# First linear of a graph kernel: the bias added by VectorE on the way out of PSUM, instead of by bias products on TensorE and copies on ScalarE

## The chip, the core and the metric

The kernel runs on 1 core of one Trainium2 chip. The metric is the device time of one execution in microseconds (us). Before the change three runs took 533.06, 533.36 and 534.27 us; their median is 533.36 us.

## The reference, cut to what matters

Four sublayers follow one another on 1250 nodes of 512 features with 40,000 edges: a graph attention with 8 heads, a gated linear with an expert picked for the whole batch, a graph convolution, and a mixture of 8 experts. The change is in the first linear of the first sublayer:

```python
def _L0_gnn_ref(x, edge_index, Ws, Wb, a_w, a_b):
    for h in range(8):
        Wx = x @ Ws[h] + Wb[h]                  # 1250 x 512 times 512 x 64, plus a bias
        s = Wx[v_tgt] @ a_w[h, :d] + Wx[v_src] @ a_w[h, d:] + a_b[h]
        s = leaky_relu(s, 0.2)
        alpha = segment_softmax(s, v_tgt, n)
        outs.append(segment_sum(alpha[:, None] * Wx[v_src], v_tgt))
...
x = x + _L0_gnn_ref(_layernorm(x), edge_index, ...)
```

## The kernel before, in words

The nodes lie in T = 10 tiles of 128. The attention needs a dense 1280 x 1280 matrix of edge counts, `C` and `C2`, and the kernel builds it first, in a loop over 160 pairs of edge chunks (20 batches `b` of LB = 8 pairs). For each pair i:

- VectorE writes one-hot matrices, for half a batch (4 pairs) at a time: `half_left` (L1033) and `half_right` (L1039), both recorded at L1019. Half u = 2b + half makes the pairs 4u to 4u+3. It may be at most 16 pairs ahead: `half_left(u)` waits until pair 4u-12 is counted.
- TensorE multiplies them in `count` (two matmuls, L1598), and `merge` (L1605) adds the old counts through the identity.
- ScalarE copies the 180 counts of a window back into `C` or `C2` (`write_batch`, L605). `merge(i)` waits for the writes of the pairs up to i-2.

The first linear is worked into this loop, one tile for every STEP = 12 pairs. Tile t begins at pair LIN_AT[t] = 16 + 12t. Before that, ScalarE normalises its rows (L574), TensorE transposes them (L1509), ScalarE copies the transposed tile as f16 at pair LIN_AT[t]-8 (L566), and VectorE makes the low part of the f16 split (`xT_low`, L938) in half LIN_AT[t]/4. In that same half VectorE calls `ln_scale` (L932, L933) for tile t+1, which waits for a square root that ScalarE takes at pair LIN_AT[t+1]-20, that is LIN_AT[t]-8 (L561). In the half after it comes `ln_stats` for tile t+2 (L915 to L917), as long as there is such a tile.

At each of the 12 pairs from LIN_AT[t] on, TensorE's `lin_a(t, j)` adds one product to two sums: 128 x 512 outputs in bank 2 + t % 2 (L1557, the values `Wx`) and 128 x 16 in bank 4 + t % 2 (L1558, the scores `sc`). Weights are scaled by WS = 256 and split into a high and a low f16 part. At j = 0 it first opens both sums with a bias product: 64 rows holding 1/32, times `Wb16` (L1553) or `cb16` (L1554), whose rows 0 to 63 hold high parts of the bias, with rows 32 to 63 turned into low parts. Before them it waits for `xT_ready` and, as the banks alternate, for `evacA` of tile t-2:

```python
                    pe.wait_ge(sem("xT_ready"), t + 1)
                    if t >= 2:
                        pe.wait_ge(sem("evacA"), t - 1)
```

At pair LIN_AT[t]+12 ScalarE takes both sums out of PSUM, in `evac_a` (L597 and L598).

The bias halves are made once. After batch 0 ScalarE writes the high parts (L677, L679, after a wait for all small loads, `ld_w1`), and after batch 1 VectorE subtracts them from the bias (L1109, L1110).

At the last batch VectorE computes `scores` (L963 to L966). TensorE transposes the thresholds at pair 146 (L1573), VectorE copies them out (L1076) behind its last one-hots, SP writes them to DRAM (L381) and reads them back broadcast (L386). When all counts are written (`hist_done`, L690) VectorE joins `C` and `C2` (L1147), and the aggregation of the heads begins; ScalarE's masks (L697) are the first to read the thresholds.

Of the kernel before, what the change touches and what calls it, by code (L numbers as in the profile page):

```python
# [8 lines left out]
F16 = mybir.dt.float16  # L9
# [59 lines left out]
ROWS_P = {LIN_AT[t] - 9: t for t in range(T)}  # L69
COPY_P = {LIN_AT[t] - 8: t for t in range(T)}  # L70
LIN_P = {LIN_AT[t] + j: (t, j) for t in range(T) for j in range(STEP)}
EVAC_P = {LIN_AT[t] + STEP: t for t in range(T)}
XT0 = 4
AHEAD = 3
EPS = 1e-5
# [3 lines left out]
def gnn_ffn_kernel(nc, x_d, src_d, dst_d, Ws_d, Wb_d, aw_d, ab_d, Wg_d, bg_d, We_d, be_d, gW_d, gb_d,  # L79
                   Wr_d, br_d, W1_d, b1_d, W2_d, b2_d, out_d):  # L80
    ctx = ExitStack()
    with ctx:
# [92 lines left out]
        ones16, o = carve(mid, o, [P], F16)  # L175
        minusT16, o = carve(mid, o, [P], F16)
        span_i, o = carve(mid, o, [2, HG], I32)
        part32, o = carve(mid, o, [2], F16)
        num_words = num[:, :, :].rearrange("p h f -> p (h f)")
        lo16, o = carve(num_words, 0, [RE], F16)  # L180
        hi16, o = carve(num_words, o, [RE], F16)
        src_i = be_bc[:, 0:RE].bitcast(I32)
        Wb16, o = carve(be_bc, 0, [D], F16)
        cb16, o = carve(be_bc, o, [2 * H], F16)
        VP, o = carve(big, 0, [T, 2, H, 2, FE], F16)
        nacc, o = carve(big, o, [T, H, FE])

# [263 lines left out]
        def _(g):  # L451
# [15 lines left out]
            nc.gpsimd.iota(iota_lo, [[1, P]], base=0, **kw)  # L467
            nc.gpsimd.memset(ones16, 1.0)
            nc.gpsimd.memset(minusT16, -float(T))
            nc.gpsimd.memset(part32, 1.0 / 32)  # L470
            nc.gpsimd.iota(iota_q, [[1, RW]], base=1, **kw).then_inc(sem("consts"), 1)
            nc.gpsimd.memset(zero[:, 0, :], 0.0).then_inc(sem("consts"), 1)
            nc.gpsimd.iota(iota8[:, :], [[1, E1]], base=-99, **kw)
# [82 lines left out]
        def _(a):  # L556
# [34 lines left out]
                if i == 3:  # L591
                    act(A2, e2t, ACT.Exp).then_inc(sem("exps"), 1)

            def evac_a(t):

                a.wait_ge(sem("linA"), t + 1)
                act(Wx[:, t, :, 0:F], bank[2 + t % 2][:, :].rearrange("p (h f) -> p h f", h=H), ACT.Copy, scale=1.0 / WS)  # L597
                act(sc[:, t, :], bank[4 + t % 2][:, 0:2 * H], ACT.Copy, scale=1.0 / WS).then_inc(sem("evacA"), 1)  # L598

            def write_batch(base, at, middle):  # L600

                for k in range(LB):
# [48 lines left out]
            for b in range(NB):  # L651
                def middle(k):
                    i = b * LB + k
                    if i in SQRT_P:
                        ln_sqrt(SQRT_P[i])
                    if i in EVAC_P:
                        evac_a(EVAC_P[i])
                    if i in NORM_P:
                        t = NORM_P[i]
                        ln_norm(t, x[:, t, :], xh_ring[:, t % 2, :])  # L660
                    if k == LB - 3 and b + 1 < NB:
                        at.append(targets(mybir.EngineType.Activation, (b + 1) * LB))
                    if b == NB - 1 and k <= 3:
                        exponential(k)
                    if b == NB - 1 and k == 4:
                        act(sd[0:1, 0:1], zero16[0:1, 0:1], ACT.Sigmoid)
                    if i in COPY_P:
                        t = COPY_P[i]
                        if t >= 2:
                            a.wait_ge(sem("linA"), t - 1)  # L670
                        ln_copy(t, bank[6], xTs[:, t % 2, 0, :, :])

                write_batch(b * LB, at[b], middle)
                if b == 0:
                    a.wait_ge(sem("wa_psum"), 1)
                    act(Wa[:, 0, :, :].rearrange("p k c -> p (k c)"), bank[5][:, 0:K * 2 * H], ACT.Copy, scale=WS)
                    act(cb16[0:64, :], bank[5][0:64, K * 2 * H:(K + 1) * 2 * H], ACT.Copy, scale=WS)  # L677
                    a.wait_ge(sem("ld_w1"), 128)
                    act(Wb16[0:64, :], Wb_bc[0:64, :, :].rearrange("p h f -> p (h f)"), ACT.Copy, scale=WS).then_inc(sem("weight_hi"), 1)  # L679
            n = a.value_load(npass[0:1, 0:1], min_val=1, max_val=MAXPASS)  # L680
            with a.If(n > 1):
                with a.Fori(1, n) as p:
# [219 lines left out]
        def _(v):  # L902
# [156 lines left out]
            def value(h):  # L1059

                if h:
                    v.wait_ge(sem("v_lo"), h)
                V.tensor_tensor(vtmp, Wx[:, :, h, :].unsqueeze(1).to_broadcast([P, 2, T, FE]),
                                bc(B12[:, :, :, h], [P, 2, T, FE]), ALU.mult).then_inc(sem("v_made"), 1)

            def tile_step(u):
                if u in SCALE_H:
                    ln_scale(SCALE_H[u])
                if u in LOW_H:
                    t = LOW_H[u]  # L1070
                    xT_low(t, bank[6], xTs[:, t % 2, :, :, :])
# [10 lines left out]
            pair_tables(0, first_stats)  # L1082
            for b in range(NB):
                if b == NB - 1:
                    scores()
                    last_onehots(b)
                    threshold_rows()
                elif b:
                    for half in range(2):
                        u = 2 * b + half  # L1090
                        if u in STATS_H:
                            if STATS_H[u] == XT0:
                                v.wait_ge(sem("ld_x"), 32)
                            ln_stats(STATS_H[u], x[:, STATS_H[u], :])
                        half_left(b, half)
                        tile_step(u)
                        half_right(b, half)
                else:
                    first_onehots()
                    ln_scale(0)  # L1100
                    v.wait_ge(sem("weight_hi"), 1)
                    V.scalar_tensor_tensor(W016[:, 1, :, :], W0.rearrange("p k h f -> p k (h f)"), WS, W016[:, 0, :, :],
                                           ALU.mult, ALU.subtract).then_inc(sem("weight_lo"), 1)
                if b == 1:
                    passes()
                    v.wait_ge(sem("weight_hi"), 2)
                    V.scalar_tensor_tensor(Wa[:, 1, :, :].rearrange("p k c -> p (k c)"), bank[5][:, 0:K * 2 * H], WS,
                                           Wa[:, 0, :, :].rearrange("p k c -> p (k c)"), ALU.mult, ALU.subtract)
                    V.scalar_tensor_tensor(cb16[32:64, :], bank[5][32:64, K * 2 * H:(K + 1) * 2 * H], WS, cb16[32:64, :], ALU.mult, ALU.subtract)  # L1109
                    V.scalar_tensor_tensor(Wb16[32:64, :], Wb_bc[32:64, :, :].rearrange("p h f -> p (h f)"), WS, Wb16[32:64, :],  # L1110
                                           ALU.mult, ALU.subtract).then_inc(sem("weight_lo"), 1)
            v.wait_ge(sem("exps"), 4)
            v.wait_ge(sem("xp_zeroed"), 16)
            V.memset(cz[:, :, NODES:NP], 0.0)
# [389 lines left out]
        def _(pe):  # L1504
# [39 lines left out]
            def lin_a(t, j):  # L1544
                k, i = divmod(j, len(PASSES))
                xp, wp = PASSES[i]
                if j == 0:
                    if t == 0:
                        pe.wait_ge(sem("weight_lo"), 2)
                    pe.wait_ge(sem("xT_ready"), t + 1)  # L1550
                    if t >= 2:
                        pe.wait_ge(sem("evacA"), t - 1)
                    mm(bank[2 + t % 2][:, :], part32[0:64, 0:1].to_broadcast([64, P]), Wb16[0:64, :], start=True, stop=False)  # L1553
                    mm(bank[4 + t % 2][:, 0:2 * H], part32[0:64, 0:1].to_broadcast([64, P]), cb16[0:64, :], start=True, stop=False)  # L1554
                xt = xTs[:, t % 2, xp, k, :]
                last = j == K * len(PASSES) - 1
                mm(bank[2 + t % 2][:, :], xt, W016[:, wp, k, :], start=False, stop=last)  # L1557
                ins = mm(bank[4 + t % 2][:, 0:2 * H], xt, Wa[:, wp, k, :], start=False, stop=last)  # L1558
                if last:
                    ins.then_inc(sem("linA"), 1)  # L1560

# [418 lines left out]
```

## Time and profile before

| | |
|---|---|
| median of 3 runs | 533.36 us (533.06 to 534.27) |
| the profiled execution | 534.08 us, of which 532.3 us are its span (first to last instruction) |
| mean granted TensorE clock | 0.979 |
| TensorE matmul busy | 486.5 us, 91% of the span |
| VectorE busy | 423.5 us, 80% |
| ScalarE busy | 341.2 us, 64% |
| GpSimd busy | 82.9 us, 16% |

The shares are means over stages with different limits. The change lies in the counting loop, between about 27 and 128 us, so that stretch has to be read by itself. PE is TensorE, PEld its weight loads, DVE VectorE, ACT ScalarE, POOL GpSimd, SP the queue that starts most transfers. A row of the timeline gives the start, the length, the engine and the line, and in brackets the idle time before it with the instruction that ended it. Successive rows of one engine may overlap by up to a tenth of a us, as the end of one instruction lies over the beginning of the next.

### The profile page before, as it was taken

Reading aid. Unit: us, or ns where it says so; the run is one execution under the profiler, and the core shown is the slowest. Engines: PE = TensorE matmul, PEld = TensorE weight load, DVE = VectorE, ACT = ScalarE, POOL = GpSimd, SP = SyncE. Lnnn points to the kernel's source line nnn. Section 1 sums busy time; section 2 is a strip of 40 time slices with the busy share of each in tenths; the row PEclk is TensorE's granted clock in tenths of the full one; section 3 lists DMA queues with packets and bytes.
Section 4 is the critical chain, followed back from the end, with each engine's and each line's share of the span. In section 5 each row is a group of like instructions: output and inputs, shape, how many; then the busy total and the mean of one; then the engine's idle time right before and its main releaser. Section 6 shows DMA issues by size and latency. Waiting matters only on the chain.

```text
span 532.3 us, 11466 instructions
## 1 busy us (share of the span) xinstructions
PE 486.5 (91%) x4389; PEld 359.9 (68%) x4390; DVE 423.5 (80%) x856; ACT 341.2 (64%) x657; POOL 82.9 (16%) x95
## 2 busy tenths in 40 slices
PE   3989999993899999999999899889899999999995
PEld 3866666762898999998787544444466697776662
DVE  7878778685999999966888778985877787886781
ACT  7467677668799999972766723435345558867630
POOL 5000000000000000001121201223244511222322
PEclk9889999999799999999999999999999999999999
DMA  8970000003011111002000294000011119965201
GB/s 201 323 262 1 1 2 1 2 2 102 2 50 52 52 54 64 37 1 80 1 2 1 89 324 161 1 0 4 0 42 42 61 60 347 379 224 184 91 28 55
DMA packets 25267, 45.10 MB, mean 85 GB/s; under 512 B 6977, under 2 KB 7013, under 8 KB 25212
## 3 DMA queue, kind: packets, MB, share of 16 engines
q1 hardware_dynamic: 23228, 39.16, 21.5%
q0 software_dynamic: 1952, 5.18, 2.7%
q8 instruction: 37, 0.61, 0.5%
q14 instruction: 18, 0.15, 0.1%
q10 hardware_dynamic: 32, 0.01, 0.0%
HBM read 33.23 MB, written 11.95 MB: 85 GB/s over the span
## 4 chain that ended last, share of the span: by engine, by line
PE 33%; DVE 21%; issue 6%; DMA 5%; ACT 4%; POOL 4%; POOLq 0%; DVEq 0%
PE sums L1697 13%; PE sums L1531 7%; PE sums L1710 5%; PE sums L1922 3%; DMA aux<-xperm_scratch 2%; POOL row L532 2%; DVE st L915 2%; DVE big L1324 2%; DMA out<-aux 2%; DVE work L1161 2%; PE sums L1509 1%; POOL out L516 1%; ACT rings L574 1%; DVE aux L1446 1%; PE sums L1687 1%
## 5 line engine op out<-in xcount | busy, mean ns | idle before, releaser
L1697 PE MATMUL sums<-big,work 128*128 128x130 f16 x1080 | 67.2, 225 | 8.0 <-DVE work L1161 7.9
L1697 PEld LDWEIGHTS sums<-big,work 128*128 128x128 f16 x1080 | 64.5, 100 | 9.6 <-issue 6.2
L1019 DVE TENSOR_TENSOR big<-mid 128x1024 f16<-128x1024 f16 (+1 forms) x88 | 59.4, 735 | 1.5 <-PE sums L1605 1.4
L1598 PE MATMUL sums<-big 128*128 128x180 f16 x320 | 59.4, 270 | 0.3 <-DVE big L1019 0.3
L1798 PE MATMUL sums<-mid 128*128 128x512 f16 x200 | 47.2, 378 | 0.0
L1710 PE MATMUL sums<-big,mid 128*128 128x260 f16 x400 | 47.0, 275 | 0.1
L1557 PE MATMUL sums<-big,rings 128*128 128x512 f16 x120 | 45.4, 378 | 0.0
L1710 PEld LDWEIGHTS sums<-big,mid 128*128 128x128 f16 x400 | 38.2, 96 | 7.5 <-issue 0.3
L605 ACT ACTIVATE mid<-sums 128x180 f32 x80 | 26.5, 332 | 25.5 <-PE sums L1605 24.8
L697 ACT ACTIVATE aux<-aux,small 128x1250 f16<-128x1250 f32 x32 | 40.9, 1326 | 2.5 <-DVE work L1161 1.7
L697 ACT ACTIVATE mid<-aux,small 128x1250 f16<-128x1250 f32 x32 | 40.8, 1324 | 2.4 <-DVE work L1161 2.4
L561 ACT ACTIVATE sd<-ve 128x1 f32<-128x1 f32 x40 | 8.0, 200 | 50.9 <-DVE ve L917 50.9
L1598 PEld LDWEIGHTS sums<-big 128*128 128x128 f16 x320 | 37.5, 120 | 3.9 <-issue 0.7
L493 POOL TENSOR_TENSOR row<-row,mid 128x512 f32<-128x512 f32 x9 | 10.6, 1177 | 162.5 <-DVE mid L1228 162.5
L915 DVE BATCH_NORM_STATS2 st<-row 128x6 f32<-128x512 f32 x40 | 27.6, 691 | 9.4 <-POOL row L532 7.8
L605 ACT ACTIVATE big<-sums 128x180 f32 x80 | 26.2, 327 | 12.9 <-PE sums L1605 11.0
L516 POOL DMA_INDIRECT out<-aux x16 | 23.1, 1446 | 70.6 <-DVE aux L1446 68.2
L1697 PE MATMUL sums<-big,rings 128*128 128x130 f16 x520 | 31.6, 220 | 0.7 <-DVE rings L1161 0.7
L574 ACT ACTIVATE rings<-row,nm,rs 128x512 f32<-128x512 f32 x30 | 24.3, 809 | 12.3 <-DVE nm L933 12.3
L1798 PEld LDWEIGHTS sums<-mid 128*128 128x128 f16 x200 | 19.7, 104 | 18.0
L1697 PEld LDWEIGHTS sums<-big,rings 128*128 128x128 f16 x520 | 29.9, 98 | 1.3 <-DVE rings L1161 1.1
L1605 PE MATMUL sums<-big,ident 128*128 x80 | 26.2, 328 | 2.9 <-ACT big L605 2.9
(330 smaller groups left out, 1099.6 us busy)
## 6 DMA issues: line engine op xcount, KB each, us to landing
big<-in_L_ffn_W SPq DMA_DIRECT2D x10, 1024.0 KB, 14.2
mid<-in_L_ffn_W SPq DMA_DIRECT2D x6, 1024.0 KB, 13.8
xperm_scratch<-work SPq DMA_DIRECT2D x1, 5753.0 KB, 18.7
aux<-thr_scratch SPq DMA_DIRECT2D x8, 640.0 KB, 3.9
aux<-xperm_scratch SPq DMA_DIRECT2D x8, 523.0 KB, 4.5
row<-in_x SPq DMA_DIRECT2D x1, 1280.0 KB
aux<-in_L_gnn_Ws SPq DMA_DIRECT2D x4, 256.0 KB, 4.6
row<-in_x SPq DMA_DIRECT2D x1, 1024.0 KB, 6.5
```

Source lines behind the costliest of these rows:

```text
L516: nc.gpsimd.indirect_dma_start(out_d, bass.IndirectOffsetOnAxis(ap=ids[0:m, r, j:j + 1], axis=0), xs[0:m, r, j, 0:D], None, bounds_check=N ...
L574: act(dst, xt, ACT.Identity, bias=nm[:, n % 2:n % 2 + 1], scale=rs[:, n % 2:n % 2 + 1]).then_inc(sem("xh_made"), 1)
L605: ins = act(counts_at(at[k], k), count_bank(base, k)[:, 0:RW].rearrange("p (d s) -> p s d", s=T), ACT.Copy)
L697: act(dst, thr_bc[:, h % 2, 0:NODES], ACT.Sigmoid, bias=steep[:, s, h:h + 1], scale=-STEEP).then_inc(sem("z_made"), 1)
L915: link(V.bn_stats(st[:, i, :], xt))
L1019: return V.tensor_tensor(out.rearrange("p c (v two) -> p c v two", two=2), values.rearrange("p (v two) -> p v two", two=2).unsqueeze(1).to ...
L1531: ins = mm(out, xt16[:, xp, k, :], w16[:, wp, k, :], start=i == 0 and k == 0, stop=i == 2 and k == K - 1)
L1557: mm(bank[2 + t % 2][:, :], xt, W016[:, wp, k, :], start=False, stop=last)
L1598: mm(count_bank(base, k)[:, 0:RW], L_ring[:, slot, k * CH + j, :], R_ring[:, slot, k * CH + j, :], start=j == 0, stop=False)
L1697: ins = mm(acc_region(h, t), weighted[i // 2 % NC][:, s % 2, t * P:(t + 1) * P], VP[:, s, part, h, :, :].rearrange("p b f -> p (b f)"), st ...
L1710: ins = mm(edge_bank(t, g2)[:, 0:4 * FE].rearrange("p (h f) -> p h f", f=FE), C[:, s, t * P:(t + 1) * P], VP[:, s, part, 4 * g2:4 * g2 + 4 ...
L1798: ins = mm(bank[6 + t % 2][:, :], C[:, s, t * P:(t + 1) * P], hp[:, s, part, :], start=s == 0 and part == 0, stop=s == T - 1 and part == 1)
```

## The change

The two bias products, `part32`, `Wb16` and `cb16` go away, and so does `evac_a` on ScalarE. ScalarE copies the score bias `cb` out of bank 5 as f32. The first product of each tile opens the sums. VectorE takes the tiles out in a new function, `linear_out`: one scalar_tensor_tensor of 128 x 512 and one of 128 x 16, each (sum x 1/WS) + bias, from PSUM to SBUF in f32.

```diff
-EVAC_P = {LIN_AT[t] + STEP: t for t in range(T)}
+EVAC_H = {(LIN_AT[t] + STEP + 16) // HALF: t for t in range(T - 1)}
...
-            def evac_a(t):
-                a.wait_ge(sem("linA"), t + 1)
-                act(Wx[:, t, :, 0:F], bank[2 + t % 2]..., ACT.Copy, scale=1.0 / WS)
-                act(sc[:, t, :], bank[4 + t % 2][:, 0:2 * H], ACT.Copy, scale=1.0 / WS).then_inc(sem("evacA"), 1)
...
                     act(Wa[:, 0, :, :]..., bank[5][:, 0:K * 2 * H], ACT.Copy, scale=WS)
-                    act(cb16[0:64, :], bank[5][0:64, K * 2 * H:(K + 1) * 2 * H], ACT.Copy, scale=WS)
-                    a.wait_ge(sem("ld_w1"), 128)
-                    act(Wb16[0:64, :], Wb_bc[0:64, :, :]..., ACT.Copy, scale=WS).then_inc(sem("weight_hi"), 1)
+                    act(cb, bank[5][:, K * 2 * H:(K + 1) * 2 * H], ACT.Copy).then_inc(sem("weight_hi"), 1)
...
+            def linear_out(t):
+                v.wait_ge(sem("linA"), t + 1)
+                V.scalar_tensor_tensor(Wx[:, t, :, 0:F], bank[2 + t % 2]..., 1.0 / WS, Wb_bc, ALU.mult, ALU.add)
+                V.scalar_tensor_tensor(sc[:, t, :], bank[4 + t % 2][:, 0:2 * H], 1.0 / WS, cb, ALU.mult, ALU.add).then_inc(sem("evacA"), 1)
...
                 if b == NB - 1:
+                    linear_out(T - 1)
                     scores()
...
                             ln_stats(STATS_H[u], x[:, STATS_H[u], :])
+                        if u in EVAC_H:
+                            if EVAC_H[u] == 0:
+                                v.wait_ge(sem("ld_w1"), 128)
+                            linear_out(EVAC_H[u])
                         half_left(b, half)
...
-                    V.scalar_tensor_tensor(cb16[32:64, :], ...)
-                    V.scalar_tensor_tensor(Wb16[32:64, :], ...).then_inc(sem("weight_lo"), 1)
...
-                    mm(bank[2 + t % 2][:, :], part32[0:64, 0:1].to_broadcast([64, P]), Wb16[0:64, :], start=True, stop=False)
-                    mm(bank[4 + t % 2][:, 0:2 * H], part32[0:64, 0:1].to_broadcast([64, P]), cb16[0:64, :], start=True, stop=False)
-                mm(bank[2 + t % 2][:, :], xt, W016[:, wp, k, :], start=False, stop=last)
-                ins = mm(bank[4 + t % 2][:, 0:2 * H], xt, Wa[:, wp, k, :], start=False, stop=last)
+                mm(bank[2 + t % 2][:, :], xt, W016[:, wp, k, :], start=j == 0, stop=last)
+                ins = mm(bank[4 + t % 2][:, 0:2 * H], xt, Wa[:, wp, k, :], start=j == 0, stop=last)
```

`EVAC_H` puts the tiles 0 to 8 at the halves 11, 14, ..., 35. Tile t's sums are thus taken out in the half that makes the pairs LIN_AT[t]+28 to LIN_AT[t]+31; in the halves 11 to 26 this stands right behind an `ln_stats`, and in all of them before the one-hots. Tile 9 is taken out just before `scores`.

## Rows read from the trace of the kernel before

**Rows 1.** Windows (us, busy us of PE, PEld, DVE, ACT, POOL, granted clock, DMA share, GB/s).
```profile
42.20:50.29 8.09, 7.74 (x68) 5.49 (x67) 6.30 (x13) 5.58 (x18) 0.00 (x0) 1.00 0.00 0
...
113.11:128.20 15.09, 10.17 (x80) 6.94 (x79) 8.79 (x25) 11.02 (x33) 0.45 (x1) 1.00 0.29 91
128.20:240.00 111.80, 101.86 (x1642) 97.30 (x1643) 106.94 (x96) 103.62 (x87) 0.00 (x0) 0.95 0.10 38
```

**Rows 2.** Timeline of PE around the bias products of tile 1.
```profile
41.56 0.38 PE L1557 MATMUL sums<-big,rings 128*128 128x512 f16 x1
...
42.20 0.39 PE L1553 MATMUL sums<-be_bc,mid 64*128 64x512 f16 x1
...
42.53 0.39 PE L1557 MATMUL sums<-big,rings 128*128 128x512 f16 x1
...
43.09 0.38 PE L1557 MATMUL sums<-big,rings 128*128 128x512 f16 x1
```

**Rows 3.** Timeline of VectorE, one tile's round and the beginning of the next.
```profile
46.19 0.16 DVE L932 RECIPROCAL rs<-sd 128x1 f32<-128x1 f32 x1 [1.56 <-ACT sd L561]
...
46.68 0.69 DVE L938 TENSOR_TENSOR rings<-sums,rings 128x512 f16<-128x512 f32 x1
47.29 0.90 DVE L1019 TENSOR_TENSOR big<-mid 128x1440 f16<-128x1440 f16 x1
48.10 0.69 DVE L915 BATCH_NORM_STATS2 st<-row 128x6 f32<-128x512 f32 x1
...
49.11 3.52 DVE L1019 TENSOR_TENSOR big<-mid 128x1024 f16<-128x1024 f16 x5
54.16 0.16 DVE L932 RECIPROCAL rs<-sd 128x1 f32<-128x1 f32 x1 [1.53 <-ACT sd L561]
...
57.08 3.52 DVE L1019 TENSOR_TENSOR big<-mid 128x1024 f16<-128x1024 f16 x5
```

**Rows 4.** Timeline of PE: the bias products of the tiles 2 and 3 begin.
```profile
50.29 0.39 PE L1553 MATMUL sums<-be_bc,mid 64*128 64x512 f16 x1
...
58.17 0.39 PE L1553 MATMUL sums<-be_bc,mid 64*128 64x512 f16 x1
```

**Rows 5.** By source line: durations (ns min/median/max) of like instructions on VectorE.
```profile
L1446 DVE SCALAR_TENSOR_TENSOR aux<-sums,small,aux x16: 735/750/753, 448.9 to 525.8; 128x512 f32<-128x512 f32 x8, 80x512 f32<-80x512 f32 x8
...
L1107 DVE SCALAR_TENSOR_TENSOR small<-sums,small x1: 225/225/225, 27.9 to 27.9; 128x64 f16<-128x64 f32 x1
```

**Rows 6.** Timeline of ScalarE and PE where tile 9's sums are taken out.
```profile
113.36 0.59 ACT L597 ACTIVATE mid<-sums 128x512 f32<-128x512 f32 x1
...
113.53 0.33 PE L1605 MATMUL sums<-mid,ident 128*128 x1
...
114.35 0.33 PE L1605 MATMUL sums<-big,ident 128*128 x1 [0.34 <-ACT big L605]
```

**Rows 7.** Timeline from the last halves to the join: VectorE, PE, SP, ScalarE; and the landing times of L386.
```profile
110.31 1.51 DVE L1019 TENSOR_TENSOR big<-mid 128x1024 f16<-128x1024 f16 x2 [0.66 <-PE sums L1605]
112.60 1.51 DVE L1019 TENSOR_TENSOR big<-mid 128x1024 f16<-128x1024 f16 x2 [0.77 <-PE sums L1605]
114.06 0.24 DVE L963 TENSOR_TENSOR small<-small 128x80 f32<-128x80 f32 x1
...
118.89 1.60 DVE L1076 COPY rings<-sums 8x512 f32<-8x512 f32 x3
...
128.16 2.30 DVE L1147 TENSOR_TENSOR mid<-mid,big 128x1280 f16<-128x1280 f16 x3 [2.04 <-ACTq L690]
...
117.77 1.25 PE L1573 MATMUL sums<-ident,small 128*8 128x128 f32 x10
...
122.46 0.81 SPq L386 DMA_DIRECT2D aux<-thr_scratch  x2
...
129.48 2.55 ACT L697 ACTIVATE mid<-aux,small 128x1250 f16<-128x1250 f32 x2
...
DMA to landing us min/median/max: 3.5/3.9/5.5
```

More of the change, by code:

```diff
@@ L177, in gnn_ffn_kernel @@
         span_i, o = carve(mid, o, [2, HG], I32)
-        part32, o = carve(mid, o, [2], F16)
         num_words = num[:, :, :].rearrange("p h f -> p (h f)")
@@ L182, in gnn_ffn_kernel @@
         src_i = be_bc[:, 0:RE].bitcast(I32)
-        Wb16, o = carve(be_bc, 0, [D], F16)
-        cb16, o = carve(be_bc, o, [2 * H], F16)
         VP, o = carve(big, 0, [T, 2, H, 2, FE], F16)
@@ L469, in _ @@
             nc.gpsimd.memset(minusT16, -float(T))
-            nc.gpsimd.memset(part32, 1.0 / 32)
             nc.gpsimd.iota(iota_q, [[1, RW]], base=1, **kw).then_inc(sem("consts"), 1)
@@ L592, in exponential @@
                     act(A2, e2t, ACT.Exp).then_inc(sem("exps"), 1)
-            def evac_a(t):
-                a.wait_ge(sem("linA"), t + 1)
-                act(Wx[:, t, :, 0:F], bank[2 + t % 2][:, :].rearrange("p (h f) -> p h f", h=H), ACT.Copy, scale=1.0 / WS)
-                act(sc[:, t, :], bank[4 + t % 2][:, 0:2 * H], ACT.Copy, scale=1.0 / WS).then_inc(sem("evacA"), 1)
             def write_batch(base, at, middle):
@@ L655, in middle @@
                         ln_sqrt(SQRT_P[i])
-                    if i in EVAC_P:
-                        evac_a(EVAC_P[i])
                     if i in NORM_P:
@@ L676, in _ @@
                     act(Wa[:, 0, :, :].rearrange("p k c -> p (k c)"), bank[5][:, 0:K * 2 * H], ACT.Copy, scale=WS)
-                    act(cb16[0:64, :], bank[5][0:64, K * 2 * H:(K + 1) * 2 * H], ACT.Copy, scale=WS)
-                    a.wait_ge(sem("ld_w1"), 128)
-                    act(Wb16[0:64, :], Wb_bc[0:64, :, :].rearrange("p h f -> p (h f)"), ACT.Copy, scale=WS).then_inc(sem("weight_hi"), 1)
+                    act(cb, bank[5][:, K * 2 * H:(K + 1) * 2 * H], ACT.Copy).then_inc(sem("weight_hi"), 1)
             n = a.value_load(npass[0:1, 0:1], min_val=1, max_val=MAXPASS)
@@ L1064, in value @@
                                 bc(B12[:, :, :, h], [P, 2, T, FE]), ALU.mult).then_inc(sem("v_made"), 1)
+            def linear_out(t):
+                v.wait_ge(sem("linA"), t + 1)
+                V.scalar_tensor_tensor(Wx[:, t, :, 0:F], bank[2 + t % 2][:, :].rearrange("p (h f) -> p h f", h=H), 1.0 / WS,
+                                       Wb_bc, ALU.mult, ALU.add)
+                V.scalar_tensor_tensor(sc[:, t, :], bank[4 + t % 2][:, 0:2 * H], 1.0 / WS, cb, ALU.mult, ALU.add).then_inc(sem("evacA"), 1)
             def tile_step(u):
@@ L1107, in _ @@
                     V.scalar_tensor_tensor(Wa[:, 1, :, :].rearrange("p k c -> p (k c)"), bank[5][:, 0:K * 2 * H], WS,
[L1108 to L1111, printed above, removed]
+                                           Wa[:, 0, :, :].rearrange("p k c -> p (k c)"), ALU.mult, ALU.subtract).then_inc(sem("weight_lo"), 1)
             v.wait_ge(sem("exps"), 4)
```

## The prediction

> **What bounds the kernel now.** I read the page's table of busy time first and only to see that no single engine is the answer: the shares mix stages. Then I cut the span into windows. The change lies between 27 and 128 us, and one tile's stretch of it, from one bias product to the next, has TensorE busy 7.74 of 8.09 us, VectorE 6.30 and ScalarE 5.58, at the full granted clock (1.00, the 2.4 GHz level) [rows 1]. So TensorE sets the pace there. The timeline of PE says how: one pair's work (one product each of L1557 and L1558, a merge, two counts) repeats every 0.56 us (42.53 to 43.09) with no gap of its own, and the one irregular step is the first of each tile, where 0.97 us pass from 41.56 to 42.53 [rows 2]. VectorE's timeline shows the opposite: once per tile it stands idle for about 1.5 us until ScalarE's square root at L561 [rows 3], and ScalarE does that in its order behind a write that waits for TensorE. VectorE is thus ahead, tied to TensorE's pace once per round, with a margin. The view of waits shows no wait of TensorE for VectorE in this stretch, and waits for ScalarE only behind pair 136. The chain that ended last is of no use here: it can be followed back only to 143 us.
>
> **The bias products.** Per tile the products of L1553 and L1554 go. From the first one's start to the first real product, 42.20 to 42.53, it is 0.33 us [rows 2]. The step as a whole is 0.97 - 0.56 = 0.41 us too long; the other 0.08 us lie before the bias product, where TensorE's queue passes the waits for `xT_ready` and `evacA`, and those stay. I take 0.33. The lower bound: a regular step moves 3 x 180 + 512 + 16 = 1068 columns in 0.56 us, so the 528 columns of the bias cost 0.28 us if only the columns count. The upper bound is 0.41. With 10 tiles: 3.3 us, between 2.8 and 4.1. Nothing covers this, because TensorE has no idle time here that it could fall into.
>
> **VectorE's new work.** Before, VectorE's round lasts 54.16 - 46.19 = 7.97 us, of which 1.53 are idle: 6.44 us of work [rows 3]. TensorE's rounds at the same place are 58.17 - 50.29 = 7.88 us and, in the window above, 8.09 us; the two kinds alternate [rows 4]. The change puts into each round one scalar_tensor_tensor of 128 x 512 from PSUM with an f32 operand in SBUF, and one of 128 x 16. The nearest rows: 0.75 us for the same operation and shape at L1446, and 0.225 us for 128 x 64 at L1107, an upper bound for 16 columns [rows 5]; L938, which also reads 512 columns of PSUM and a second tensor, has 0.69 [rows 3]. Successive instructions on VectorE overlap by about 0.08 us (0.69 from 46.68, but the next starts at 47.29). So the pair takes 0.75 - 0.08 + 0.225 - 0.08 = 0.81 us of the round, between 0.7 (by L938) and 0.98 (no overlap). The round's work becomes 7.25 us against a round of TensorE of 7.97 - 0.33 = 7.64. VectorE still arrives early, by 0.39 us, and the work is hidden by that idle time. If that cover were gone, each us over it would be added to the round.
>
> **The new wait on TensorE.** This is the place where the change can bite. `lin_a` of tile t+2 waits for `evacA` of tile t, which ScalarE gave one whole round earlier and VectorE now gives late. For the tiles 0 to 5 VectorE reaches `linear_out` behind `ln_stats`. In the old timeline that is 49.11 us, where the one-hots now start, and TensorE wants the bank at 50.29; in the next round it is 57.08 and 58.17 [rows 3, 4]. Both are counted from the same ScalarE step, with no bias product between, so the distances (1.18 and 1.09 us) stay. The pair is done 0.75 - 0.08 + 0.225 = 0.90 us after it starts. That leaves 0.28 and 0.19 us, less some hundredths for the semaphore and 0.08 because TensorE's queue handles its waits just before. I count no wait, and at most 0.1 us for each of 6 tiles. Queued behind such a wait are the next merges and counts, so all of the loop would be late with it. The tiles 6 to 8 have no `ln_stats` before them and are 1.0 us better off. The wait of `linear_out` itself, on `linA`, is on a sum that was finished a round before (tile 0 at 42.2 us, read at 49.1), so it stops nobody; at tile 9 the sum is finished at 113 us and VectorE comes after 114.
>
> **ScalarE.** It loses 10 times 0.59 us and a small copy. In the rounds it had idle time, so that gives nothing, except at tile 9: there the write of a window waits behind L597 from 113.36 on, and the merge at 114.35 stands idle for 0.34 us [rows 6]. That goes: -0.34. The copies of the bias halves go also (ScalarE once 0.63 and 0.17 us after batch 0, VectorE about 0.8 us after batch 1), at a point where VectorE waits over 2 us for the round behind it: nothing.
>
> **The end of the loop.** VectorE takes tile 8 and tile 9 out just where its idle times are 0.66 and 0.77 us. The tiles 7 and 8 cost 1.62 us and use these up, and tile 9 another 0.81: scores start about 1.0 us late, 1.3 counted from the pair on TensorE that is 0.33 us earlier, and 1.7 if the 0.34 at tile 9 comes too. Scores began at 114.06, the first thresholds are ready half a us later, and TensorE asks for them only at 117.77, so 3.2 us of cover are enough. VectorE copies the thresholds out after its last one-hots, now up to 1.7 us late; the load issued at 122.46 lands 3.5 to 5.5 us later, as a rule 3.9, so with the delay at 128.1, and the first mask that reads it starts at 129.48 (129.1 after the gain at tile 9). Hidden, by 1.0 us. What follows, the join at 128.16, waits for the last write of ScalarE alone, and VectorE is then busy 106.94 of 111.80 us [rows 7, 1]: each us won before the join is won at the end.
>
> **The sum.** -3.3 - 0.34 = -3.64 us. On the profiled execution that is 534.08 - 3.64 = 530.44 us (span 528.7); it lay 0.72 us above the median, so for the median 533.36 - 3.64 = 529.7 us.
>
> **A rule that speaks against it.** The Trainium skill, in Perfetto Trace Analysis, section Optimizing Scalar/DVE Operations, gives VectorE a larger fixed cost on PSUM (about 125 ns) than ScalarE (about 51 ns) and advises to shift work to ScalarE where VectorE is saturated. The trace agrees on the first point (0.69 to 0.75 us against 0.59), and by the rule the change goes the wrong way: VectorE is the busier of the two. Were VectorE saturated, the gain would shrink as in the first rival below.
>
> **The rivals.**
> - *VectorE becomes the bound of the round.* It needs a pair of 1.20 us (7.64 - 6.44), against 0.98 at the worst from rows. For it speaks only that the margin shrinks from 1.5 to 0.4 us. Then the rounds with statistics keep about their old length and only tiles 0, 1, 8 and 9 and the 0.34 give anything: 4 x 0.33 + 0.34 = 1.7 us, 531.7. Chance 0.07.
> - *TensorE waits for the bank in six tiles.* The margin is 0.1 to 0.2 us by my reckoning. If the pair takes 0.2 us longer, or the semaphore does, TensorE loses about 0.1 to 0.25 us six times, 0.6 to 1.5 us: 530.3 to 531.2. Chance 0.15.
> - *The thresholds come late.* The first load of L386 is the one that lands after 5.5 us: then it is there at 129.7, 0.6 us after the mask wants it: 530.3. With a further us of delay 531.3. Chance 0.05.
> - *The products were covered after all:* the step's length is that of the waits, and TensorE only stands there instead. For it: the queue's 0.08 us. Against it: 0.33 us between two product starts. Only 0.34 us are left, 533.0, no measurable change. Chance 0.05.
> - *Slower: the wait for the bank, large.* Same place as the second, but the pair of 0.9 us slips by a whole one-hot product or more (0.90 us, L1019), or VectorE is slowed in PSUM while TensorE writes other banks. From 0.79 us a tile on, six times, it eats the 3.64 us and 1.07 more; at 0.9 us of wait the time is 533.36 - 3.64 + 5.4 = 535.1. Against it: L938 reads PSUM in the midst of TensorE's writes in 0.69 us, the same every time. Chance 0.06.
>
> **How the numbers follow.** The forecast itself has 0.62, with its own range from 528.4 (4.1 for the bias, 0.34, and half a us from ScalarE's free time elsewhere) to 530.6 (2.8). To hold 8 in 10 the range takes in the second and third rival and the first: 528.2 to 531.9 us. A measurement of this kernel tells about 0.2% from no change, 1.07 us. Faster by more than that, below 532.3 us, are the forecast and the first three: 0.89, of which I take 0.04 away for what I have not thought of: 0.85. Within it 0.08, slower 0.07.
>
> **What would show it.** In the profile after: the round of TensorE 7.55 and 7.76 us instead of 7.88 and 8.09; L1557 of each tile starting where L1553 did, with no idle time before it that ends on VectorE; the new operations on VectorE at about 0.75 and 0.2 us; VectorE's idle time before L932 at 0.3 to 0.5 us instead of 1.53; no idle time of 0.34 us near tile 9; the join at about 124.5 instead of 128.16 us, and everything after it the same length. Wrong it would be if TensorE shows a wait on the new line's semaphore in the tiles 2 to 7, if VectorE has no idle time left before L932, if ScalarE's first mask waits for a load, or if the stretch behind the join has grown.

## The result, and the profile after

The changed kernel takes 532.0 us (median of 20 runs, 527.97 to 535.06). In the same measurement the kernel before, of which three runs had given 533.36, came to 536.95 us over 20 runs (533.06 to 539.18). The ratio is 0.9922, with a 95% interval from 0.9899 to 0.9945: 4.2 us less, between 3.0 and 5.4. (The means over all runs, 531.99 and 536.16 us, give this ratio; the two medians lie 4.95 us apart.) The forecast difference was 3.64 us. The forecast time of 529.7 us was 2.3 us too low, and 532.0 lies 0.1 us above the upper end of the range.

The profiled execution of the changed kernel took 533.77 us with a span of 532.0 us, only 0.3 us less than before. Each trace is one execution: that of the kernel before (534.08 us) was among its faster ones, that of the changed kernel among its slower ones. One has to look where those 532.0 us lie. First the windows of the changed kernel, from its merge 16 (the pair at which tile 0 begins) to the join and from the join to the end; columns as in [rows 1].

```profile
36.71:126.90 90.19, 83.11 (x717) 60.77 (x716) 75.67 (x153) 59.79 (x178) 0.45 (x1) 1.00 0.05 16
126.90:532.00 405.10, 377.21 (x3518) 278.45 (x3518) 326.83 (x655) 256.89 (x421) 73.63 (x66) 0.98 0.23 82
```

The same two stretches of the kernel before:

```profile
33.86:128.16 94.30, 86.83 (x736) 61.65 (x736) 68.73 (x132) 65.12 (x198) 0.45 (x1) 1.00 0.07 24
128.16:532.30 404.14, 376.76 (x3518) 278.37 (x3518) 327.06 (x655) 256.72 (x421) 74.62 (x66) 0.98 0.23 82
```

The loop behind merge 16 became 4.11 us shorter (94.30 to 90.19). VectorE has 6.9 us more work in it, ScalarE 5.3 less. But merge 16 came 2.85 us later (36.71 instead of 33.86), in a stretch that the change hardly touches, and the rest behind the join took 1.0 us more. So there are two questions: why the loop won 4.1 us, and what the first 37 us do.

Timeline of PE in the changed kernel, last step of tile 0 and the first steps of tile 1, which answers to [rows 2]:

```profile
43.98 0.38 PE L1550 MATMUL sums<-big,rings 128*128 128x512 f16 x1
...
44.53 0.38 PE L1550 MATMUL sums<-big,rings 128*128 128x512 f16 x1
...
45.32 0.38 PE L1550 MATMUL sums<-big,rings 128*128 128x512 f16 x1
...
45.87 0.38 PE L1550 MATMUL sums<-big,rings 128*128 128x512 f16 x1
```

The first step of the tile, 43.98 to 44.53, takes 0.55 us, as every other: all of the 0.42 us are gone, the 0.08 before the bias product too. The step after it takes 0.79 us (44.53 to 45.32); more on that in experiment 5.

Timeline of VectorE in the changed kernel, one round with statistics (L918 is L932 of before, L924 is L938, L1005 is L1019), which answers to [rows 3]:

```profile
56.31 0.69 DVE L924 TENSOR_TENSOR rings<-sums,rings 128x512 f16<-128x512 f32 x1
56.92 0.90 DVE L1005 TENSOR_TENSOR big<-mid 128x1440 f16<-128x1440 f16 x1
57.74 0.68 DVE L901 BATCH_NORM_STATS2 st<-row 128x6 f32<-128x512 f32 x1
...
58.74 0.68 DVE L1055 SCALAR_TENSOR_TENSOR mid<-sums,aux 128x512 f32<-128x512 f32 x1
59.34 0.16 DVE L1057 SCALAR_TENSOR_TENSOR small<-sums,small 128x16 f32<-128x16 f32 x1
59.42 3.52 DVE L1005 TENSOR_TENSOR big<-mid 128x1024 f16<-128x1024 f16 x5
63.55 0.16 DVE L918 RECIPROCAL rs<-sd 128x1 f32<-128x1 f32 x1 [0.60 <-ACT sd L557]
```

The pair of L1055 and L1057 pushes the one-hots from 58.74 to 59.42, 0.68 us and not 0.81: the large operation has 0.68 and not 0.75 us, the small one 0.16 and not 0.225. VectorE still waits for ScalarE's square root, 0.60 us here and 0.42 in the next round, where it was 1.53 to 1.56. TensorE's sums were done long before, and no product of TensorE waits for L1057.

The end of the loop in the changed kernel, timeline of VectorE, SP and ScalarE, which answers to [rows 7]:

```profile
113.31 0.68 DVE L1055 SCALAR_TENSOR_TENSOR mid<-sums,aux 128x512 f32<-128x512 f32 x1
113.91 0.16 DVE L1057 SCALAR_TENSOR_TENSOR small<-sums,small 128x16 f32<-128x16 f32 x1
114.11 0.24 DVE L949 TENSOR_TENSOR small<-small 128x80 f32<-128x80 f32 x1
...
126.90 2.29 DVE L1142 TENSOR_TENSOR mid<-mid,big 128x1280 f16<-128x1280 f16 x3 [2.05 <-ACTq L676]
...
122.51 0.81 SPq L383 DMA_DIRECT2D aux<-thr_scratch  x2
...
128.22 2.55 ACT L683 ACTIVATE mid<-aux,small 128x1250 f16<-128x1250 f32 x2
```

The scores begin 12.8 us before the join; before the change it was 14.1. The delay of 1.3 us is at the lower end of the 1.3 to 1.7 that I had counted. The thresholds' load starts 4.4 us before the join instead of 5.7, and the first mask still has no idle time ahead of it.

### The profile page after: what moved, and what is told of

It is laid out like the page before. It is cut to its first block, busy times and chain, and to the rows that moved or that the text cites. A ratio compares the mean times of both kernels' runs of the same rounds, so it can differ in the third digit from the quotient of the medians.

```text
span 532.0 us, 11423 instructions
## 1 busy us (share of the span) xinstructions
PE 486.3 (91%) x4369; PEld 361.9 (68%) x4370; DVE 429.0 (81%) x874; ACT 335.7 (63%) x636; POOL 81.9 (15%) x94
## 4 chain that ended last, share of the span: by engine, by line
PE 36%; DVE 20%; DMA 5%; issue 5%; POOL 4%; ACT 3%; POOLq 0%; DVEq 0%
PE sums L1690 13%; PE sums L1526 7%; PE sums L1703 5%; PE sums L1915 4%; DMA out<-aux 2%; DMA aux<-xperm_scratch 2%; DVE st L901 2%; POOL row L528 2%; PE sums L1886 2%; DVE work L1156 1%; PE sums L1504 1%; DVE big L1319 1%; POOL out L512 1%; PE sums L1680 1%; ACT rings L570 1%
## 5 line engine op out<-in xcount | busy, mean ns | idle before, releaser
L1005 DVE TENSOR_TENSOR big<-mid 128x1024 f16<-128x1024 f16 (+1 forms) x88 | 59.4, 732 | 0.0
L1690 PE MATMUL sums<-big,rings 128*128 128x130 f16 x520 | 31.8, 220 | 0.7 <-DVE rings L1156 0.7
## 6 DMA issues: line engine op xcount, KB each, us to landing
mid<-in_L_ffn_W SPq DMA_DIRECT2D x6, 1024.0 KB, 14.1
```

The lines of the kernel that those rows point to most:

```text
L1005: return V.tensor_tensor(out.rearrange("p c (v two) -> p c v two", two=2), values.rearrange("p (v two) -> p v two", two=2).unsqueeze(1).to ...
L1690: ins = mm(acc_region(h, t), weighted[i // 2 % NC][:, s % 2, t * P:(t + 1) * P], VP[:, s, part, h, :, :].rearrange("p b f -> p (b f)"), st ...
```

## The experiments

Times are medians, with the number of runs; "loop" is the time from merge 16 to the join in the trace (94.30 us before, 90.19 after), "start" the time until merge 16 (33.86 and 36.71). The kernel before was run beside each group: 536.75 us in the first (35 runs), 536.78 in the second (23), 536.89 in the third (16). The ratio to the kernel before is again not the quotient of the two medians. Loop and start are read from one trace of each version.

**1. The bias products alone left out of the kernel before.** The bias of the first linear is then missing from the result.

```diff
-                    mm(bank[2 + t % 2][:, :], part32..., Wb16[0:64, :], start=True, stop=False)
-                    mm(bank[4 + t % 2][:, 0:2 * H], part32..., cb16[0:64, :], start=True, stop=False)
-                mm(bank[2 + t % 2][:, :], xt, W016[:, wp, k, :], start=False, stop=last)
-                ins = mm(bank[4 + t % 2][:, 0:2 * H], xt, Wa[:, wp, k, :], start=False, stop=last)
+                mm(bank[2 + t % 2][:, :], xt, W016[:, wp, k, :], start=j == 0, stop=last)
+                ins = mm(bank[4 + t % 2][:, 0:2 * H], xt, Wa[:, wp, k, :], start=j == 0, stop=last)
```

> The kernel before with the two bias products of each tile left out, and with them the bias of the first linear; ScalarE still takes the tiles out and the halves of the bias are still made. My theory, that the gain of the change is TensorE's: the first step of a tile becomes 0.55 us instead of 0.97, ten times, less about 0.1 us in the odd tiles, so 3.7 us (0.7%) less than before, and TensorE's idle time of 0.34 us at tile 9 stays. Rival, that moving the work from ScalarE to VectorE carries a good part of it: less than 2.5 us here.

Measured: 531.67 us (12 runs), ratio 0.9932 (0.9902 to 0.9962). Loop 90.33 us, 3.97 less than before; start 32.92. The first steps are 0.55 us in the tiles 1 to 9. The gain is TensorE's, nearly all of it, and the rival falls.

**2. VectorE takes the tiles out, the bias products stay** (the changed kernel with the lines of before for `part32`, `Wb16`, `cb16` and the two products put back; the bias is thus added twice).

> The changed kernel with the bias products and the halves put back on TensorE (the bias is thus added twice): only the move from ScalarE to VectorE is left of the change. My theory: VectorE hides it, the gap at tile 9 goes, so 0.3 to 0.5 us less than before, not to be told from no change; rounds of VectorE keep an idle time near 0.8 us. Rival, the move costs: VectorE is late for TensorE and the time is 1 us or more above before.

Measured: 536.37 us (12 runs), ratio 0.9976 (0.9938 to 1.0013), not to be told from no change; the trace decides here. Loop 94.06 us, 0.24 less than before; first steps 0.97 us as before. VectorE is busy 75.83 us in this loop against 68.73 before, and that costs nothing. The parts add up: 3.97 + 0.24 = 4.21 us, against 4.11 for both together.

**3. The tile taken out twice by VectorE.**

```diff
             def linear_out(t):
                 v.wait_ge(sem("linA"), t + 1)
+                V.scalar_tensor_tensor(gW[:, t % 4, :], bank[2 + t % 2][:, :], 1.0 / WS, Wb_bc..., ALU.mult, ALU.add)
                 V.scalar_tensor_tensor(Wx[:, t, :, 0:F], ..., 1.0 / WS, Wb_bc, ALU.mult, ALU.add)
```

> The changed kernel with one more scalar_tensor_tensor of 128 x 512 per tile on VectorE, into free memory, ahead of the real one (0.61 us of VectorE's round each). By my reckoning the margin before TensorE asks for the bank is 0.2 to 0.4 us, so TensorE waits 0.2 to 0.4 us in six tiles and the time is 1 to 2.5 us above the changed kernel, that is 1.7 to 3.2 below the kernel before. Rival, the margin is wider than I worked out (VectorE's idle time only shrinks): equal to the changed kernel, 4 us below before.

Measured: 534.51 us (12 runs), ratio 0.9971 (0.9938 to 1.0004), 2.5 us above the changed kernel. Loop 93.27 us, 3.08 longer than with one. The view of waits names it (who waited for whom: us in total, times, longest), L1551 being the first product and L1058 the small operation of `linear_out`:

```profile
PE sums L1551 <- DVE small L1058: 1.8, 6, 0.4
```

Six waits, in the tiles 2 to 7, exactly those that stand behind statistics. Their first steps are 0.95 to 1.06 us instead of 0.55: 0.40 to 0.51 us late for 0.60 us more work. (The view counts only part of that: the six steps are 2.8 us longer together, and it has 1.8.) So the changed kernel had a margin of 0.1 to 0.2 us there and no more. VectorE itself was not the bound, it still had idle time before L918 (0.60 and 0.24 us).

**4. Each tile taken out half a batch later.**

```diff
-EVAC_H = {(LIN_AT[t] + STEP + 16) // HALF: t for t in range(T - 1)}
+EVAC_H = {(LIN_AT[t] + STEP + 20) // HALF: t for t in range(T - 1)}
```

> The changed kernel with each tile taken out half a batch later (halves 12, 15, ..., 36), 1.5 us later in VectorE's order. By the doubled take-out the margin before TensorE is 0.1 to 0.2 us in tiles 2 to 7 and 1.0 us wider in tiles 8 and 9: so TensorE waits 1.3 us in six tiles and 0.3 in two, 8 us in all: from merge 16 to the join 98 us and not 90.2, and the whole 4 us above the kernel before. Rival, a late TensorE also lets VectorE catch up, and the wait settles at half of that: 94 us.

Measured: 541.38 us (10 runs), ratio 1.0088 (1.0055 to 1.0122). Loop 98.91 us, 8.7 longer than in the changed kernel. Waits, and the first step of tile 2 in the timeline of PE:

```profile
PE sums L1550 <- DVE small L1057: 6.7, 6, 1.2
```

```profile
53.59 0.38 PE L1550 MATMUL sums<-big,rings 128*128 128x512 f16 x1 [1.08 <-DVE small L1057]
```

The first steps are 1.74 to 1.88 us in the tiles 2 to 7 and 0.79 in the tiles 8 and 9, together 8.1 us over 0.55. VectorE does not catch up: its wait for ScalarE's square root, 0.40 to 0.61 us in the changed kernel from 55 us on, is now 1.65 to 2.02 us, so it stays tied to TensorE's pace. This is how the change turns into a loss: the same edit, put 1.5 us later in VectorE's order.

**5. TensorE's address loads one pair later.**

```diff
-                    if k == LB - 3 and b + 1 < NB:
+                    if k == LB - 2 and b + 1 < NB:
                         later = targets(mybir.EngineType.PE, (b + 1) * LB)
```

> The changed kernel with TensorE's load of the next batch's window addresses moved from behind the sixth pair of a batch to behind the seventh. The rounds of the odd tiles begin at the fifth pair of a batch, and in the trace of the change the second step of those tiles takes 0.79 to 0.83 us, where the bias product had covered the loads. My theory: this step falls to about 0.6 us, and 0.1 us a tile comes back in five tiles, 0.5 us from merge 16 to the join (90.2 us to 89.7), not to be told in the time. Rival, the gap is the price of the semaphore waits at the tile's first step: the 0.8 us stay.

Measured: 532.66 us (12 runs), ratio 0.9906 (0.9869 to 0.9943). In the timeline of PE, the steps of tile 1, where the second had been 0.79 us:

```profile
44.53 0.38 PE L1550 MATMUL sums<-big,rings 128*128 128x512 f16 x1
...
45.08 0.38 PE L1550 MATMUL sums<-big,rings 128*128 128x512 f16 x1
...
45.71 0.38 PE L1550 MATMUL sums<-big,rings 128*128 128x512 f16 x1
```

The second step is 0.55 us now, in all five odd tiles, and part of the gap moved to the third (0.63). The gap was thus the loads', not the semaphores'. The trace of the changed kernel fits: in tile 1 the load runs on TensorE's queue from 44.68 to 45.27 us, and the weights of the next product follow at 45.29; before the change it ran from 42.10 to 42.69, beside the bias products. But the time from a tile's first step to its last rose from 6.89 to 7.03 us in most even tiles, and the loop is 90.50 us, not 89.7: the explanation held, the gain did not come.

**6. The start: statistics of the first tile behind the one-hots,** so that the first counts do not wait for the load of x.

```diff
-            pair_tables(0, first_stats)
+            pair_tables(0)
...
                     first_onehots()
+                    first_stats()
-                    ln_scale(0)
                     v.wait_ge(sem("weight_hi"), 1)
                     V.scalar_tensor_tensor(W016[:, 1, :, :], ...)
+                    ln_scale(0)
...
-            ln_sqrt(0)
...
+                    if i == 3:
+                        ln_sqrt(0)
```

> The changed kernel with the first tile's statistics moved on VectorE from before the tables of pairs to behind the first one-hots, and its square root on ScalarE from before the loop to pair 3: the first counts no longer wait for the load of x. Theory A, that the spread of the executions comes from TensorE's clock level in the first 35 us and not from the load as such: the first merge comes at 16.4 us in every trace, up to 1.2 us earlier than where the load is late, yet the runs still lie 4 us or more apart and the median is only 0 to 1.5 us below the changed kernel's. Theory B, that the late load is the cause of the long start, directly and through the clock: the runs draw together to about 3 us and the median falls to 529 to 530.

Measured: 530.06 us (6 runs, 529.55 to 533.16), ratio 0.9892 (0.9843 to 0.9941). The trace is that of the slowest of the six runs: here no instruction waits for x, and still the start takes 36.68 us, as the changed kernel's 36.71, though the first merge came at 17.12 us (17.55 there; I had expected 16.4). The late load is not needed for a long start. TensorE stays at its lower level until 33.0 us here and until 35.4 us there. By the times, neither theory is clean: the median fell by 1.9 us, more than theory A had said, four of the six runs lie within 1 us, and a spread of 3.6 us remained.

**7. TensorE kept busy in the start.** Products of zeros, 400 columns each: six before the first weights arrive, three before the first counts, one after each of the first six pairs.

```diff
+            for _ in range(6):
+                mm(bank[1][:, 0:400], zero16[:, 0:P], zero16[:, 0:400], start=True, stop=True)
             pe.wait_ge(sem("ld_w0"), 16 * K)
...
             w0_T(3)
+            for _ in range(3):
+                mm(bank[5][:, 0:400], zero16[:, 0:P], zero16[:, 0:400], start=True, stop=True)
...
+                if b == 0 and k <= K + 1:
+                    mm(bank[3][:, 0:400], zero16[:, 0:P], zero16[:, 0:400], start=True, stop=True)
```

> The changed kernel with products of zeros on TensorE in the first 25 us: six of 400 columns before the first weights arrive, three before the first counts, and one after each of the first six pairs. Theory on the missed level: the executions differ because TensorE runs the first 35 us at the lower of its two clock levels for a time that varies from one execution to the next; kept busy, it reaches the full level before 18 us in every execution and keeps it. Then the eight small products of one block of weights take 0.99 us and not 1.79, the loop's pair 16 is reached 2 to 5 us earlier, the median is 5 to 8 us below before and the runs lie within 2 us of each other. Rival, the spread is from the arrival of the inputs: the products of zeros cost 1 to 2 us and the spread stays at 5 us or more.

Measured: 529.52 us (12 runs, 528.24 to 533.68), ratio 0.991 (0.9878 to 0.9942). Start 31.81 us. Nine of the runs lie between 528.2 and 531.2, three at 533.2 to 533.7. The start is 4.9 us shorter than in the changed kernel's trace, but not in every execution. The time is 7.2 us below the kernel before, as my theory had it; the spread of 5.4 us is not the 2 us that it had, nor did the level hold (lower from 25.1 to 28.5 us).

**8. The edits 5, 6 and 7 together.**

> The changed kernel with the products of zeros of the first 25 us, the later first statistics and the later address loads together. If the start is TensorE's clock above all: median 528 to 529 us, 8 us below the kernel before, and no run above 531. If the products of zeros only add work where the clock falls anyway: 530 or more, and runs at 533 as with them alone.

Measured: 528.15 us (6 runs, 527.24 to 528.72), ratio 0.9849 (0.9802 to 0.9896). Start 31.14, loop 91.20 us. This version beats both kernels, and its six runs lie within 1.5 us.

**9 and 10. The kernel before and the changed kernel, both with these three edits, on one chip.**

> The kernel before the change with the same three edits of the start: products of zeros, later first statistics, later address loads. If the start's clock made both the level and the spread, and the change only shortens the loop, this kernel lies 4.1 us above the changed one with the same edits (528.2 + 4.1 = 532.3 us) with runs within 2 us, and merge 16 to the join takes 94 to 95 us. Rival, the change also moves the start: the distance is 2 us or 6 us instead, and merge 16 comes elsewhere than at 31 us.

> The changed kernel with the three edits once more, on the chip of this call, to stand beside the kernel before with the same edits: 528.2 us, runs within 2 us, merge 16 near 31 us.

Measured: 532.20 us (11 runs, 531.45 to 533.26) and 528.35 us (6 runs, 527.60 to 529.90); ratios to the kernel before 0.9926 (0.99 to 0.9951) and 0.9854 (0.9817 to 0.9891). Starts 31.84 and 31.34 us, loops 94.88 and 91.35. With the start kept busy in both, the change is worth 3.85 us of median, and of that the traces show 3.53 in the loop and 0.5 in the start. The loops are longer than without the edits (94.30 and 90.19); in the changed kernel tile 0 takes 8.71 us to the next tile instead of 7.50, so a part of what the start gains is given back there.

**11. Only the nine products before the loop,** with the later statistics and the later address loads.

> The same without the six products of zeros inside the first batch, so that only the nine before the loop remain. If it is the small f32 products of the first batch (16 columns each) that let the clock fall, the level drops again near 21 us and merge 16 comes at 32.5 to 34 us: 530 us, with a spread of 3 us or more. Rival, what counts is to start the loop at the full level: 528 us, as with all.

Measured: 528.23 us (6 runs, 527.11 to 530.44), ratio 0.9852 (0.9813 to 0.9891). Start 31.32 us. Windows of the stretch from 21 to 31 us: in this kernel,

```profile
21.00:31.00 10.00, 6.95 (x57) 5.30 (x57) 9.69 (x25) 4.63 (x16) 0.00 (x0) 1.00 1.01 369
```

in the kernel before,

```profile
21.00:31.00 10.00, 9.79 (x52) 8.68 (x52) 7.73 (x20) 4.45 (x15) 0.00 (x0) 0.52 1.05 379
```

and in the changed kernel:

```profile
21.00:31.00 10.00, 9.79 (x50) 9.05 (x50) 5.33 (x12) 2.54 (x9) 0.00 (x0) 1.00 1.04 379
```

(The clock of 1.00 in the last row is not a measured one, see below.) In this kernel TensorE does more in that stretch with 6.95 us busy than the others with 9.79, because like products take about half the time (0.99 for 1.79 us), and the six products inside the batch are not needed. The level did not drop in this trace and the median is the rival's; six runs, with one at 530.44 us, say little of the spread.

## Why the prediction was right in its steps and wrong in its time

**The step that failed is the base of the sum.** "It lay 0.72 us above the median, so for the median 533.36 - 3.64 = 529.7 us" took three runs for the level of the kernel, and the range took in only the costs of the change. Over more runs the kernel before has its median at 536.8 to 536.95 us, and single runs from 532.2 to 539.8. The three that I had (533.06 to 534.27) were from the lower part. With 536.95 as the base the same sum gives 533.3 us, 1.3 above the measured 532.0; the range should have had some 3.6 us on its upper side for the base alone. What was forecast of the change itself, 3.64 us, lies within the interval of the measured 4.2, though in part by luck, as the terms below show.

**What makes the level differ is the start.** Over the thirteen traces, one execution each, the part behind the join takes 403.5 to 405.1 us; the loop follows the edit (90.2 to 91.4 us for all versions without bias products and waits); the start goes from 31.1 to 37.3 us, and not by the edit, as long as TensorE is not kept busy:

| kernel | start (us) | TensorE's clock in the start |
|---|---|---|
| before | 33.86 | full level from 17.9 to 21.3 us, then the lower one to 31.6 |
| after | 36.71 | lower level until 35.4 |
| products left out (1) | 32.92 | full from 13.5 to 20.4, lower to 30.6 |
| move to VectorE alone (2) | 37.30 | full from 13.4 to 16.8, lower to 33.9 |
| taken out twice (3) | 37.29 | full from 13.2 to 16.6, lower to 33.7 |
| address loads later (5) | 36.64 | lower until 33.6 |
| half a batch later (4) | 36.86 | lower until 35.0 |
| statistics later (6) | 36.68 | lower until 33.0 |
| kept busy (7) | 31.81 | full from 11.5 to 25.1, lower to 28.5 |
| all three (8) | 31.14 | full from 13.3 to 30.4, lower to 33.8 |
| before with all three (9) | 31.84 | full from 11.7 to 25.3, lower to 28.7 |
| all three again (10) | 31.34 | full from 11.1 to 24.8, lower to 28.2 |
| nine products only (11) | 31.32 | full from 17.5 on |

The two levels are 1.2 and 2.4 GHz. Where the table begins with the lower one, the trace has no record of the clock before the time given, and the level is read from the length of the products. What they cost is seen at the eight small f32 products of one block of weights, in the timeline of PE. The kernel before:

```profile
20.36 0.99 PE L1624 MATMUL sums<-aux,rings 128*128 128x16 f32 x8
...
21.64 1.79 PE L1624 MATMUL sums<-aux,rings 128*128 128x16 f32 x8
```

The changed kernel, in which all five such blocks take 1.79 us:

```profile
23.12 1.79 PE L1617 MATMUL sums<-aux,rings 128*128 128x16 f32 x8
```

Here TensorE sets the pace of the first batch, so 0.80 us a block, and more at the counts, go into the start. How many of the five blocks take 1.79 us orders all thirteen starts: none in 7 to 11 (31.1 to 31.8 us), two in the kernel before and in 1 (33.86 and 32.92), all five in the other six (36.6 to 37.3). That the clock level is the cause of the long starts is shown by the experiments that keep TensorE busy (7 to 11: in 8 to 11 the 6 to 11 runs of each lie within 1.5 to 3.3 us; 7 alone had three of twelve runs at 533 us and above). That it also makes the spread of the times fits the single runs, of which only the mean granted clock is known: the seven fastest of the changed kernel (527.97 to 531.03 us) all have 0.977 to 0.980, the thirteen others (from 531.85 us on) 0.983 to 0.988, as the traced one with its unrecorded start, or 0.970 and 0.971. In the kernel before the two groups are not so clean.

The traces leave a rival: the two short starts without products of zeros are both of kernels built on the one before (before and 1), the six long ones all have the take-out on VectorE. Does the change itself lengthen the start? The times speak against it: the loop lost 4.1 us and the means of all runs 4.2, which leaves nothing for a start that is longer as a rule; experiment 1 (531.67 us) lies 0.3 us from the changed kernel (532.0); and with the start kept busy in both (9 and 10) merge 16 comes at 31.84 and 31.34 us. What decides in a given execution whether the level rises at 13, at 18 or only at 35 us is not shown. In all the long starts in which VectorE waits for x, its load landed late (first statistics at 14.1 us and later in 2, 3 and after, 13.8 in 4, 13.5 in 5, instead of 12.7 in before and 1), which fits a longer idle time of TensorE before its first counts; experiment 6 has no such wait and the level stayed low all the same.

**The bias products:** "I take 0.33", 3.3 us. Measured 0.42 a tile, 4.2 us, just above my upper bound of 0.41. The 0.08 us before the bias product, which I had left to the semaphore waits, went also. Experiment 1 keeps both waits and has the short step, so the 0.08 us were not their price; what they were is not shown. What I had not seen is that the bias product covered something, which the prediction put at nothing. Where the next batch's addresses are loaded, the second step of the odd tiles grew from 0.56 to 0.80 to 0.83 us (0.64 in tile 9); their fifth step, in which the next tile is transposed, fell from about 1.51 to 1.39. The net is 0.54 us over all (9 tiles: 77.96 us from the first product of tile 0 to the last of tile 9 became 74.72, that is 3.24 and not 9 x 0.42 = 3.78). So the loop's 4.1 us are 4.2 for the bias, less 0.54 for what it had covered, and 0.45 at tile 9. That my 3.3 and the net 3.7 agree is partly luck: a term too small and a term left out. (The prediction also calls the first step "the one irregular step"; the fifth is irregular too, before and after.)

**VectorE's work hidden by its idle time:** right, and cheaper than counted (0.68 for 0.81 us). "By 0.39 us" early; measured 0.40 to 0.61.

**"I count no wait, and at most 0.1 us":** right, the trace shows none. The margin that I put at 0.28 and 0.19 us less 0.1 is 0.1 to 0.2 by experiment 3. The rival with the large wait was the right one to fear: experiment 4 shows it, 8.7 us for 1.5 us of delay.

**Tile 9's idle time, 0.34 us:** from the last product of L1557 to the join it was 15.60 us and is 15.15, 0.45 less; experiment 2, which has only this part of the gain, shows 0.24. Right within a tenth or two.

**"Each us won before the join is won at the end":** right. The part behind the join varies by 1.7 us over all traces, with no tie to how early the join came; the changed kernel's 405.1 is the longest, and its versions with TensorE kept busy in the start have 403.8 to 404.2.

**The signs that I named:** rounds of TensorE 7.55 and 7.76 us; measured 7.44 to 7.50 and 7.77 to 7.84 us from tile to tile. The join "at about 124.5 instead of 128.16": it came at 126.90, and there the start had already shown that it was off by 2.85 us.

## What to carry to other kernels

Before a sum is set on a level, look at what makes the level: three runs that agree within a quarter of a per cent can all be from one side of a spread of 7 us, and a stretch that TensorE runs now at one clock level and now at the other is where to look for it. Here a take-out of PSUM moved to an engine with idle time at no cost because it was done before the bank was wanted, and its place in that engine's order matters more than its length: 0.6 us more work cost 0.5 us a tile, 1.5 us later cost 1.3 us a tile, and both began to cost once a margin of 0.1 to 0.2 us was used up. Where TensorE spends its start at the lower clock level, products of zeros in its idle time can be worth about as much as the change under study: nine of them, with the later statistics and the later address loads, took 3.8 us off the median here. The nine were not measured alone; the later statistics by themselves had 530.06 us, 1.9 less than the changed kernel, and fifteen products by themselves 529.52.

## What the runs showed of the hardware that was not expected

- A bias product of 64 rows and 512 columns with its 16-column neighbour cost 0.42 us in a stream of TensorE in which a pair's whole work takes 0.55 us; taken out, the step became exactly as long as any other.
- The granted clock of a window is not enough to tell the level in the start. In the changed kernel the row of 21 to 31 us says 1.00, and yet the products in it take 1.79 us for 0.99: the trace has no record of the clock before 35.4 us. The Trainium skill, in TensorE: Matmul & The Clock Gate, Part 1, warns that these clock records are not always to be trusted, and the trace agrees; the durations of like products have to be compared.
- TensorE was busy for 9.79 of the 10 us from 21 to 31 us in the changed kernel and stayed at the lower level; with nine products of zeros before the loop (and the two other edits) it had the full one from 17.5 us on, in the one trace of that kernel.
- VectorE read 512 columns of PSUM, scaled, added a second f32 tensor and wrote strided f32 in 0.68 us, less than the same operation with a scale per partition at L1446 (0.75); that the scale is what differs is not shown.
